# Aggregation of a graph network: addresses of DVE's additions computed one group ahead, one of four one-hot matrices made on DVE

## What is computed

```python
w = ex / denom[dst]                                          # softmax weights, 4 heads an edge
agg = jax.ops.segment_sum(w[:, :, None] * V[src], dst, num_segments=N)
```

## Time and profile before

| | |
|---|---|
| median of three runs | 7085.9 us (7082.45 to 7089.11) |
| span of the profiled execution, first to last instruction | 6353.0 us |
| busy in it: PE / DVE / ACT / POOL | 4654.9 / 4416.1 / 2770.5 / 4352.2 us |
| additions of the aggregation (line 1048) | 1664, 706.8 us |
| matmuls of the aggregation (line 1060) | 3328, 830.3 us |
| multiplications of POOL (line 1008) | 416, 786.5 us |
| distances / encodings of ACT (lines 1017, 1030) | 530.0 / 300.3 us |

### The profile page before, as it was taken

One profiled execution on the slowest core, in us unless ns is written; L12 is line 12 of the kernel. 1 busy time (PEld: TensorE's weight loads), 2 busy tenths in 40 slices (PEclk: granted clock), 3 DMA queues, 4 the chain that ended last, 5 costly groups with the idle time before them and its releaser, 6 DMA issues. The chain is left out here.

```text
span 6353.0 us, 69502 instructions
## 1 busy us (share of the span) xinstructions
PE 4654.9 (73%) x16402; PEld 3170.3 (50%) x16402; DVE 4416.1 (70%) x8998; ACT 2770.5 (44%) x6174; POOL 4352.2 (69%) x4103
## 2 busy tenths in 40 slices
PE   9877878787777777378888879966666666666662
PEld 5565666565666666256666644433333333343331
DVE  8867888888887777867777779945555555555557
ACT  2144444444444444288888847722222222222222
POOL 0067777777777777188787835567777777777773
PEclk9977677777777777599999989977877877767775
DMA  4489999999999999177777723355555665555554
GB/s 149 127 301 338 330 340 340 335 336 335 337 350 341 372 362 367 57 235 223 222 222 222 223 88 102 96 155 158 158 157 157 159 157 157 158 157 158 159 157 135
DMA packets 925700, 1418.46 MB, mean 223 GB/s; under 512 B 93803, under 2 KB 699235, under 8 KB 924985
## 3 DMA queue, kind: packets, MB, share of 16 engines
q1 hardware_dynamic: 705209, 749.70, 37.1%
q0 software_dynamic: 213088, 657.94, 33.4%
q10 hardware_dynamic: 7010, 6.38, 0.3%
HBM read 1140.54 MB, written 273.11 MB: 223 GB/s over the span
## 5 line engine op out<-in xcount | busy, mean ns | idle before, releaser
L653 POOL DMA_INDIRECT s_rows<-kv_rows,other x1664 | 1712.8, 1029 | 507.3 <-issue 471.1
L1401 POOL DMA_INDIRECT t_rows<-xj_rows,other x1664 | 1598.9, 961 | 523.0 <-issue 468.9
L1460 PE MATMUL ps_xsum<-t_rows,t_att 128*128 128x256 f32 x3328 | 1325.8, 550 | 783.2 <-DVE t_att L1426 783.0
L1460 PEld LDWEIGHTS ps_xsum<-t_rows,t_att 128*128 128x128 f32 x3328 | 787.3, 263 | 1321.3 <-DVE t_att L1426 1195.4
L1426 DVE SCALAR_TENSOR_TENSOR t_att<-iota,local,t_att 128x128 f32<-128x128 f32 x1664 | 579.0, 348 | 1037.9 <-ACT t_att L1416 1037.9
L1416 ACT ACTIVATE t_att<-t_att,t_rows 128x128 f32<-128x128 f32 x1664 | 531.2, 389 | 1571.4 <-DMA t_rows<-xj_rows,other 1563.9
L764 PE MATMUL ps_q<-node_tab,hot 128*128 x3328 | 1162.4, 510 | 0.0
L664 ACT ACTIVATE apart<-apart,minus_p 128x1024 bf16<-128x1024 bf16 x416 | 477.6, 1148 | 1221.5 <-DMA apart<-what_rows 1221.4
L1060 PE MATMUL ps_sum<-a_terms,a_hot 128*128 128x260 f32 x3328 | 830.3, 392 | 167.5 <-DVE node_tab L1048 155.0
L762 PE MATMUL ps_rel<-rel,hot 64*128 64x64 f32 x3328 | 583.3, 329 | 495.1 <-ACT hot L669 453.8
L1008 POOL TENSOR_TENSOR a_terms<-a_terms,score 128x1024 f32<-128x1024 f32 x416 | 786.5, 1902 | 193.4 <-DMA a_terms<-v_edges 191.5
(11 more groups left out here) (206 smaller groups left out, 3554.9 us busy)
## 6 DMA issues: line engine op xcount, KB each, us to landing
v_edges<-s_rows SPq DMA_DIRECT2D x416, 512.0 KB, 6.5
a_terms<-v_edges SPq DMA_DIRECT2D x416, 512.0 KB, 4.4
apart<-what_rows SPq DMA_DIRECT2D x416, 256.0 KB, 8.3
t_att<-a_rows SPq DMA_DIRECT2D x416, 256.0 KB, 3.5
s_rows<-kv_rows,other POOLq DMA_INDIRECT x1664, 6.0
t_rows<-xj_rows,other POOLq DMA_INDIRECT x1664, 3.2
kv_rows<-kv_out SPq DMA_DIRECT2D x97, 256.0 KB, 2.0
xj_rows<-n_hx SPq DMA_DIRECT2D x97, 130.0 KB, 2.3
```

Source lines behind the costliest of these rows:

```text
L653: pool.indirect_dma_start(out=rows[g % KV_RING][:, k, :], out_offset=None, in_=t["kv_rows"], in_offset=bass.IndirectOffsetOnAxis(ap=t["oth ...
L1401: pool.indirect_dma_start(out=rows[g % RING][:, k, :], out_offset=None, in_=t["xj_rows"], in_offset=bass.IndirectOffsetOnAxis(ap=t["other1 ...
L1460: nc.tensor.matmul(ps_sum[g % 4][:, k, :], att[g % ATT_RING][:, k, :], rows[g % RING][:, k, 0:D], start=True, stop=True)\
```

## The change

- `sums_of(g)` loads the block numbers of group g and lowers the four operand addresses at once (`lower_ap`). It is called for group 0 ahead of the loop, and for group g + 1 after the second addition of group g; the additions then use the finished addresses.
- `encode_last(g)` makes the fourth one-hot of group g on DVE in one instruction: the constant row 0..127 is compared with the edge's number (`tensor_scalar`, is_equal, fp32, 128x128, SBUF to SBUF). The first three are made ahead of the loop, that of group g + 3 after the first addition of group g. Made for group g, it waits until PE has finished group g - 4, the previous reader of its buffer.
- ACT makes three distances instead of four, and encodes 384 columns instead of 512.
- PE waits for one more semaphore, `last_hot`, before each group.
- The 22 semaphores of the softmax stage join the list that POOL clears at the start of the aggregation.

```diff
@@ softmax_numerators
         def sem(name):
-            return ctx.enter_context(nc.semaphore(name))
+            t["spent"].append(ctx.enter_context(nc.semaphore(name)))
+            return t["spent"][-1]
@@ aggregate
-        far = [sb(f"a_far{u}", [P, U, P], bf16) for u in range(3)]
+        far = [sb(f"a_far{u}", [P, U - 1, P], bf16) for u in range(3)]
+        last_hot = sem("a_last_hot")
@@ scalar
-                for k in range(U):
+                for k in range(U - 1):
                     at = g * U + k
                     last = nc.scalar.activation(far[g % 3][:, k, :], t["iota"][:, :], ACT.Abs, scale=-1.0, bias=t["local0"][:, at:at + 1])
-                nc.scalar.activation(hot[g % 4][:, :, :], far[g % 3][:, :, :], ACT.Relu, scale=-1.0, bias=t["ones"][:, 0:1]).then_inc(hot_ready, 1)
+                nc.scalar.activation(hot[g % 4][:, 0:U - 1, :], far[g % 3][:, :, :], ACT.Relu, scale=-1.0, bias=t["ones"][:, 0:1]).then_inc(hot_ready, 1)
@@ vector
+            def sums_of(g):
+                sums = [tab[:, bass.ds(block * AW, AW)] for block in blocks_of(nc, dve, t["places0"], g)]
+                for acc in sums:
+                    dve.lower_ap(acc)
+                return sums
+
+            def encode_last(g):
+                at = g * U + U - 1
+                if g >= 4:
+                    dve.wait_ge(summed, g - 3)
+                dve.tensor_scalar(hot[g % 4][:, U - 1, :], t["iota"][:, :], t["local0"][:, at:at + 1], None, ALU.is_equal).then_inc(last_hot, 1)
+
+            for g in range(3):
+                encode_last(g)
+            sums = sums_of(0)
             for g in range(G):
-                blocks = blocks_of(nc, dve, t["places0"], g)
                 dve.wait_ge(summed, g + 1)
-                for k in range(U):
-                    acc = tab[:, bass.ds(blocks[k] * AW, AW)]
+                for k, acc in enumerate(sums):
                     if g * U + k:
                         dve.wait_ge(added, g * U + k)
                     dve.tensor_tensor(acc, acc, ps_sum[g % 2][:, k, 0:AW], ALU.add).then_inc(added, 1)
+                    if k == 0 and g + 3 < G:
+                        encode_last(g + 3)
+                    if k == 1 and g + 1 < G:
+                        following = sums_of(g + 1)
+                sums = following
             dve.wait_ge(added, G * U)
@@ tensor
                 pe.wait_ge(hot_ready, g + 1)
+                pe.wait_ge(last_hot, g + 1)
                 pe.wait_ge(weights_put, g + 1)
```

## The result

| | before | after |
|---|---|---|
| median | 7087.5 us (4 runs, 7082.5 to 7090.5) | 7217.7 us (4 runs, 7187.1 to 7242.4) |
| ratio | 1 | 1.0196, 95% interval 1.0177 to 1.0215 |
| aggregation, first to last addition | 984 us, 2.366 a group | 1130 us, 2.716 a group |

The change makes the kernel 130 us slower, and it does so in the aggregation: +146 us in the profiled execution. The forecast was 7135 us, with a range to 7195. The direction and the mechanism were right; the loss is two to three times the forecast one, and the time lies above the range.

What follows compares the result with a forecast made beforehand. DVE's chain of additions was taken as the bound, 2.34 a group. With comparisons waiting for POOL, the period goes from 2.366 to 2.48 over 416 groups, +47.4, with the clears +48.9: 7135 us, 8-in-10 range 6962 to 7195.

Steps and rivals of the forecast that it cites:

- Part 1: Aggregation: table load and four addresses move a group ahead, costed at nothing; 0.143 gaps between dependent additions become 0.04.
- the loop of the two PSUM buffers: Aggregation: PE 1.99, 0.07, four additions with the comparison 1.89, 0.15; together 4.10 for two groups, 2.05 each.
- some 0.15: Aggregation, DVE: us the early address work would add if the sequencer should not run ahead of the waits.
- The comparison's length: Aggregation, DVE: a 128-column comparison takes 0.28 us, about 0.10 more than the gap it fills.
- The clears: Start of the aggregation: POOL clears 22 more semaphores at 0.07 each, 1.5 us on the stage's start.
- The collision: Aggregation: a comparison meeting POOL's running multiplication waits for its end, additions behind it too; stage +47.4 us.
- Rival a: Aggregation: no collision, or comparisons stay in POOL's gaps; period 2.05 plus 0.03, 6968 us, -1.7%; chance 0.18.
- four periods, 2.46 each: Aggregation: the loop from group k's comparison to group k+4's takes 9.83 us, so 2.46 a group, taken as 2.48.
- rival c: Aggregation slower still: POOL's second slip, three periods of 3.3 in part, up to 7300, or slower PE clock, 7185; chance 0.11.
- the clock: Aggregation: PE's clock falls with its busy share, 0.12 on each period, 7185 us; part of a 0.11 chance.
- The length of the loop: Aggregation: comparison end through additions, PE, load and POOL's multiplication to the end of a later comparison, 9.83 us.
- the 733 us: Whole kernel: median 7085.9 lies 732.9 above the profiled span of 6353.0; this rest was taken as constant.

Runs made afterwards that it cites:

- paired: Changed kernel, with POOL starting group g's multiplication only behind the comparison of group g - 1: ratio to before 0.9879, stage 890.3 us, period 2.140.
- addresses_only: Kernel before plus only the addresses a group ahead, all four one-hots still on ACT: ratio to before 0.9854, 6971 against 7074 us, period 2.101.
- row_in_psum_free: Changed kernel, comparison reading the constant row from PSUM, order kept by a PE wait instead of a DVE wait: ratio to before 0.9841, stage 879.7 us.

## Why the prediction was right and wrong

- **What bounds before** was right: DVE's chain. The stage is 984 us in both profiles of before.
- **Part 1** was right in kind, and its steps of 0.46 came. But the work of the sequencer, costed at nothing, is not hidden: without a blocked comparison it puts 1.11 between the first and the third addition of a group. DVE's chain is then 2.10 instead of the 1.99 of the sum, and not the loop of the two PSUM buffers (2.05) but this chain binds still. The 0.11 lies near the prediction's own "some 0.15" for this case. It has no part in the forecast: where a comparison waits for POOL, the sequencer works meanwhile (the addition behind the next one follows after 0.45), and the measured terms of the loop are those of the sum.
- **The comparison's length**, 0.28, and its end 0.09 behind POOL's were right. Its own cost, taken as 0.10, is nothing: unblocked groups have 2.10 with it and without it, as it fits into the sequencer's time.
- **The clears** cost what was said: 88 of them run from 3147.2 to 3153.4 us, 6.2 instead of the 4.6 of 66.
- **The collision** was right, as the dose of POOL's work (1.90, 1.04, 0.30), the PSUM input and the order in paired each show. Rival a, no collision, with 0.18, fell; the stage would have been near 880.
- **The step that failed** is the count of periods in the loop, "four periods, 2.46 each". The prediction read it from the kernel before, where POOL works eight groups ahead, and took it as fixed. In the changed kernel POOL is nine groups ahead, the loop three periods, for 100 to 170 us at a time and in about half of the stage (160 comparisons against 146): the mean of 2.72 lies between 2.45 and 3.04. What came is rival c, "a second slip, three periods of 3.3, in part of the stage", which had 0.11 together with the clock; the measured 3.04 is below its 3.3 because loads land sooner there. With the whole stage at four periods it would be about 1020 to 1030 us and the forecast right, by this case's numbers. The length of the loop was right (9.7 against 9.83), the clock (1.00) had no part.
- Slow stretches load less (0.55 of the DMA time against 0.66 to 0.68), so loads land sooner, 3.7 instead of 4.2. The load's time isn't a constant of the loop, as the prediction took it, but moves with the period.
- **The base**: the 733 us were not time outside the span, as the prediction took them, without consequence here.
- What makes POOL slip from four periods to three and back is open. A load that comes early enough lets POOL start one multiplication more before DVE's comparison; this is argued, not shown. Three and four periods both hold themselves up for many groups.

## What to carry to other kernels

Before filling an engine's gaps with work, look at what else its operands' path serves: here an SBUF to SBUF comparison of DVE waited for the end of a running GpSimd multiplication, an operation with two SBUF inputs did so in the earlier trace rows, and the in-order work behind waited too. The additions, with one input in PSUM, did not. If it must stand there, take one input from PSUM, cut the GpSimd operation in pieces, or tie GpSimd's start to the end of the DVE operation. When a blocked step feeds back into the time of its blocker, list every number of periods that the loop can lock to, and price each: the likeliest one is not the mean. And when a gap moves, ask between which two operations it lies: a row of four additions need not be one group.

The best of these kernels leave the comparison out or its row in PSUM: addresses_only 0.9854 (0.9838 to 0.9870), row_in_psum_free 0.9841 (0.9819 to 0.9863), not to be told apart. The early addresses are the whole gain.

## What the runs showed of the hardware

- A comparison of 128 fp32 columns took 0.278 from SBUF and 0.345 from PSUM; the first waited for POOL's tensor_tensor up to 1.75 us (2.03 - 0.28), the second never: 413 of them took 142.7 us together.
- In the profile such a wait is inside the instruction's length (0.28 to 2.03 for one shape) and in no wait row. The spread between least and median is the sign to look for.
- On DVE an addition that waits for the one before starts 0.034 us after its end when its address is ready (0.143 in the kernel before); a load of four block numbers by the sequencer takes 0.34, and with four addresses 0.57, and the next operation of the queue waits for it.
- PE started each group 0.146 after the last addition that frees its buffer. Gaps of 0.11 stand in no bracket and no wait row of these views, though each is a wait.
